# A decoder layer on one core: the first batches and the ternary weights get a list of steps of their own on each engine

## The reference

```python
# 1: linear attention without a denominator, 16 heads of 32
q, k, v = x @ Wq.T + bq, x @ Wk.T + bk, x @ Wv.T + bv
phi_q, phi_k = elu(q) + 1.0, elu(k) + 1.0
context = phi_q * cumsum(phi_k * v, axis=1) * 32 ** -0.5
x = layernorm(x + context @ Wo.T + bo)
# 2: attention over ctx, 32 query heads on 8 key heads of 16; ctx is keys and values
x = layernorm(x + softmax(qh @ kh.T / 4) @ vh)
# 3: feed-forward, 512 -> 2048 -> 512, each of its three products being
def h_bitlinear(x, w):
    xq = act_quant(fwht(x))      # Walsh-Hadamard, then 8 bits per token
    wq = weight_quant(w)         # scale = mean(|w|); round(w / scale) in -1, 0, 1, times scale
    return xq @ wq.T
x = layernorm(x + h_bitlinear(silu(h_bitlinear(x, w_gate)) * h_bitlinear(x, w_up), w_down))
```

## Time and profile before

| what | value |
|---|---|
| median of the runs | 1795.86 us |
| lowest and highest of three runs | 1795.64 and 1796.21 us |
| the profiled execution, its own time | 1794.42 us |
| its span, first to last instruction | 1792.6 us |
| PE busy | 1629.8 us (91% of the span) |
| DVE, ACT, POOL busy | 1379.0, 833.8, 186.6 us |
| granted PE clock, mean | 0.961 of full speed |
| one round of the cyclic order, steady | 100.36 us |
| issue of w_gate's transfer | 6.75 us after the start |

### The profile page before, as it was taken

One profiled execution on the slowest core, in us unless ns is written; L12 is line 12 of the kernel. 1 busy time (PEld: TensorE's weight loads), 2 busy tenths in 40 slices (PEclk: granted clock), 3 DMA queues, 4 the chain that ended last, 5 costly groups with the idle time before them and its releaser, 6 DMA issues.

```text
span 1792.6 us, 25396 instructions
## 1 busy us (share of the span) xinstructions
PE 1629.8 (91%) x10470; PEld 1006.7 (56%) x10470; DVE 1379.0 (77%) x1759; ACT 833.8 (47%) x784; POOL 186.6 (10%) x154
## 2 busy tenths in 40 slices
PE   7776699999999999999999999999999999996855
PEld 5443465655656565655656565655656565653534
DVE  3776897878869697878869697878879697877746
ACT  1134336363554545463544546463645536453623
POOL 0402502001020202010010202010010202010000
PEclk9886699999999999999999999999999999997978
DMA  5432220404050311404040311304040401304000
GB/s 206 64 99 106 38 19 19 63 19 62 2 80 1 62 19 30 52 20 62 2 80 1 71 11 33 48 19 63 9 73 1 74 8 40 42 7 60 7 6 12
DMA packets 100122, 75.73 MB, mean 42 GB/s; under 512 B 6044, under 2 KB 85148, under 8 KB 99496
## 3 DMA queue, kind: packets, MB, share of 16 engines
q1 hardware_dynamic: 100008, 74.10, 22.4%
...
## 4 chain that ended last, share of the span: by engine, by line
PE 81%; DVE 9%; ACT 7%; issue 2%; DMA 1%; SPq 0%; POOL 0%; POOLq 0%; ACTq 0%; DVEq 0%
PE psum L658 11%; PE psum L508 11%; PE psum L685 7%; PE psum L702 6%; PE psum L532 6%; PE psum L554 6%; PE psum L609 6%; PE psum L596 5%; PE psum L575 5%; ACT ffn_mem L733 3%; PE psum L677 3%; PE psum L638 2%; PE psum L542 2%; ACT qdT L733 2%; PE psum L694 2%
## 5 line engine op out<-in xcount | busy, mean ns | idle before, releaser
L736 ACT ACTIVATE attn_mem<-psum 128x1024 f32<-128x1024 f32 x256 | 254.8, 1023 | 137.3 <-PE psum L609 135.3
L1013 DVE TENSOR_REDUCE mneg<-psum 128x4 f32<-128x1024 f32 x256 | 303.6, 1218 | 14.1 <-PE psum L575 13.7
L733 ACT ACTIVATE ffn_mem<-psum 128x1024 f32<-128x1024 f32 x160 | 160.4, 1023 | 245.6 <-PE psum L677 100.6
L1144 POOL TENSOR_TENSOR grstd<-gvare,neg_half 128x1 f32<-128x1 f32 x32 | 18.2, 568 | 1376.3 <-DVE gvare L912 1376.3
L575 PE MATMUL psum<-kst,attn_mem 96*128 96x256 bf16 x1024 | 152.2, 277 | 7.6 <-DMA attn_mem<-q_dram 3.0
L609 PE MATMUL psum<-attn_mem,kst 98*128 98x512 bf16 x512 | 150.2, 390 | 7.6 <-ACT ffn_mem L733 2.9
L824 ACT ACTIVATE ffn_mem<-psum,sc 128x1024 f32<-128x1024 f32 x64 | 71.4, 1115 | 183.3 <-PE psum L658 183.1
L1105 DVE TENSOR_TENSOR ffn_mem<-ffn_mem 128x1024 f32<-128x1024 f32 x128 | 150.4, 1215 | 0.6
L685 PE MATMUL psum<-had,ffn_mem 128*128 128x128 f32 x1024 | 129.2, 280 | 16.5 <-ACT ffn_mem L733 16.5
L596 PE MATMUL psum<-attn_mem,vpad 128*32 128x256 f32 x2048 | 141.1, 394 | 3.3 <-ACT attn_mem L736 3.3
L685 PEld LDWEIGHTS psum<-had,ffn_mem 128*128 128x128 f32 x1024 | 121.9, 194 | 30.0 <-issue 18.1
(11 more groups left out here) (152 smaller groups left out, 2501.7 us busy)
## 6 DMA issues: line engine op xcount, KB each, us to landing
attn_mem<-q_dram SPq DMA_DIRECT2D x192, 128.0 KB, 6.7
...
x_in<-in_x SPq DMA_DIRECT2D x16, 512.0 KB, 3.9
...
ffn_mem<-in_L_ffn_w_gate SPq DMA_DIRECT2D x1, 4096.0 KB, 21.6
ffn_mem<-in_L_ffn_w_up SPq DMA_DIRECT2D x1, 4096.0 KB, 13.9
ffn_mem<-in_L_ffn_w_down SPq DMA_DIRECT2D x1, 4096.0 KB, 13.9
c_in<-in_ctx SPq DMA_DIRECT2D x16, 128.0 KB, 2.2
```

The source lines that it names most:

```text
L733: return nc.scalar.activation(dst, src, ACT.Copy)
L736: return nc.scalar.activation(dst, src, ACT.Exp, **kw)
L1013: nc.vector.tensor_reduce(mneg[:, h, t, GQ * g:GQ * (g + 1)], region(f"max{u}").rearrange("p (h t) -> p h t", h=GQ), AX_X, ALU.max, negate ...
```

## The change

`orders` is unchanged. Two tables of lists are new, `first_orders` and `last_orders`, and `all_batches` runs the cyclic order only for i = 3 to 15 between them. In `first_orders` an entry names its batch directly (`x_k.1+1` is batch 1, no suffix is batch 0); in `last_orders` it is counted from the last batch. All steps run exactly as often as before. `last_orders` spells out what the cycle did in rounds 16 to 19, in the same sequence on every engine. `first_orders` is another sequence than that of the rounds up to 2.

```diff
-    LEAD = 4
+        first_orders = {
+            "sp": """x_fetch t_load.0 x_fetch+1 x_split x_stack.0 t_load.1 x_stack.1 s_mT.0 t_load.2 s_mT.1 x_fetch+2 x_split+1
+                x_stack.0+1 x_stack.1+1 s_mT.0+1 s_mT.1+1""",
...
+            "dve": """t_abs.0 x_k.1 x_v.1 x_q.3 x_ctx x_o.1 x_norm t_sum.0 x_split t_quarter.0.0 x_q2 t_lower.0.1 t_quarter.0.1
...
+            "pool": """x_prep s_copy x_o.1""",
+        }
+        last_orders = {
...
-            for i in range(-LEAD, B + LEAD):
+            for entry in first_orders[engine].split():
+                n, name, args = parsed(entry)
+                steps[name](n, *args)
+            for i in range(3, 16):
                 for off, name, args in steps_of[engine]:
                     n = i + off
                     if n == 0 or (0 < n < B and name[0] != "t"):
                         steps[name](n, *args)
+            for entry in last_orders[engine].split():
+                off, name, args = parsed(entry)
+                steps[name](B - 1 + off, *args)
```

More of the change, by code:

```diff
@@ L192, in decoder_layer @@
                 s_copy-2 c_dn.0-3 c_dn.1-3""",
+        }
+        first_orders = {
+            "sp": """x_fetch t_load.0 x_fetch+1 x_split x_stack.0 t_load.1 x_stack.1 s_mT.0 t_load.2 s_mT.1 x_fetch+2 x_split+1
+                x_stack.0+1 x_stack.1+1 s_mT.0+1 s_mT.1+1""",
+            "pe": """x_load x_k.0 x_v.0 x_q.0 x_k.1 x_q.1 x_v.1 x_q.2 x_q.3 x_c x_o.0 x_o.1 t_sum.0 x_split x_load+1 x_kst.0 x_k.0+1
+                x_k.1+1 x_v.0+1 t_quarter.0.0 x_v.1+1 x_kst.1 s_max.0 t_quarter.0.1 s_max.1 s_max.2 s_max.3 s_max.4 s_max.5
+                s_max.6 s_max.7 x_q.0+1 s_mT.0 x_q.1+1 s_max.8 x_q.2+1 s_max.9 s_max.10 s_scores.0 x_q.3+1 t_quarter.0.2 x_c+1
+                s_scores.1 t_quarter.0.3 s_scores.2 x_o.0+1 s_scores.3 x_o.1+1 s_max.11 s_max.12 t_sum.1 s_pv.0 s_max.13
+                s_max.14 s_max.15 s_scores.4 s_scores.5 s_scores.6 s_pv.1 s_scores.7 s_mT.1 t_quarter.1.0 s_pv.2 t_quarter.1.1
+                s_pv.3 s_scores.8 s_scores.9 s_scores.10 s_scores.11 s_pv.4 s_scores.12 t_quarter.1.2 s_scores.13 s_scores.14
+                s_out.0 s_pv.5 s_scores.15 s_pv.6""",
+            "act": """x_load x_k.1 x_q.3 x_split x_load+1 x_q1 x_k.1+1 t_quarter.0.0 x_kst.0 x_kst.1 t_quarter.0.1 s_mT.0 s_scores.0
+                x_q.3+1 t_quarter.0.2 s_scores.1 t_quarter.0.3 s_scores.2 s_scores.3 s_scores.4 s_scores.5 s_mT.1 s_scores.6
+                t_quarter.1.0 s_scores.7 t_quarter.1.1 s_scores.8 s_scores.9 s_scores.10 s_scores.11 s_scores.12 t_quarter.1.2
+                s_scores.13 s_scores.14 s_scores.15 x_load+2 t_quarter.1.3 t_quarter.2.0 x_split+1 t_quarter.2.1 t_quarter.2.2
+                t_quarter.2.3 x_q1+1 d_hT x_k.1+2 x_kst.0+1 d_hx d_round d_qx c_gate.0 c_gate.1 c_gate.2 s_mT.0+1 c_gate.3
+                x_kst.1+1 x_q.3+2 c_dT.0.0""",
+            "dve": """t_abs.0 x_k.1 x_v.1 x_q.3 x_ctx x_o.1 x_norm t_sum.0 x_split t_quarter.0.0 x_q2 t_lower.0.1 t_quarter.0.1
+                x_k.1+1 t_lower.0.3 t_quarter.0.2 x_v.1+1 s_max.0 t_quarter.0.3 s_max.1 s_max.2 s_max.3 s_max.4 s_max.5 s_max.6
+                s_max.7 s_mT.0 s_max.8 s_max.9 x_q.3+1 x_ctx+1 s_max.10 t_abs.1 x_o.1+1 t_sum.1 s_max.11 s_pv.0 s_max.12
+                s_max.13 s_max.14 s_max.15 t_quarter.1.0 s_pv.1 t_lower.1.1 s_mT.1 t_quarter.1.1 t_lower.1.3 t_quarter.1.2
+                t_quarter.1.3 s_pv.2 s_pv.3 s_pv.4 s_out.0 s_pv.5""",
+            "pool": """x_prep s_copy x_o.1""",
+        }
@@ new lines, in decoder_layer @@
+        last_orders = {
+            "sp": """c_store.0-2 x_split x_stack.0 c_store.1-2 x_stack.1 s_mT.0 s_mT.1 c_store.0-1 c_store.1-1 c_store.0 c_store.1""",
+            "pe": """s_pv.7-2 x_load s_out.1-2 x_split-1 x_k.0 x_k.1 x_kst.0-1 d_hT-2 d_hx-2 x_v.0 x_v.1 d_qx-2 s_max.0-1 s_max.1-1
+                s_max.2-1 c_gate.0-2 s_max.3-1 c_up.0-2 s_max.4-1 c_gate.1-2 s_max.5-1 s_max.6-1 c_up.1-2 s_max.7-1 x_q.0
+                c_gate.2-2 c_up.2-2 x_q.1 s_mT.0-1 c_gate.3-2 x_kst.1-1 x_q.2 x_q.3 s_max.8-1 c_up.3-2 c_dT.0.0-2 s_scores.0-1
+                x_c s_scores.1-1 c_H.0.0-2 c_dT.0.1-2 s_max.9-1 c_H.0.1-2 s_max.10-1 s_scores.2-1 x_o.0 s_scores.3-1 x_o.1
+                s_max.11-1 c_dT.1.0-2 c_dT.1.1-2 s_max.12-1 s_pv.0-1 c_H.1.0-2 s_max.13-1 c_H.1.1-2 s_scores.4-1 s_max.14-1
+                s_scores.5-1 s_max.15-1 c_q.0-2 s_scores.6-1 s_mT.1-1 s_pv.1-1 c_dn.0-2 s_scores.7-1 s_pv.2-1 c_q.1-2 s_pv.3-1
+                s_scores.8-1 s_scores.9-1 s_scores.10-1 c_dn.1-2 s_scores.11-1 s_pv.4-1 s_scores.12-1 s_scores.13-1 s_pv.5-1
+                s_scores.14-1 s_out.0-1 s_scores.15-1 s_pv.6-1 s_pv.7-1 s_out.1-1 x_split x_kst.0 d_hT-1 d_hx-1 d_qx-1 s_max.0
+                s_max.1 s_max.2 c_gate.0-1 s_max.3 c_up.0-1 s_max.4 c_gate.1-1 s_max.5 s_max.6 c_up.1-1 s_max.7 c_gate.2-1
+                c_up.2-1 s_mT.0 c_gate.3-1 x_kst.1 s_max.8 c_up.3-1 c_dT.0.0-1 s_scores.0 s_scores.1 c_H.0.0-1 c_dT.0.1-1
+                s_max.9 c_H.0.1-1 s_max.10 s_scores.2 s_scores.3 s_max.11 c_dT.1.0-1 c_dT.1.1-1 s_max.12 s_pv.0 c_H.1.0-1
+                s_max.13 c_H.1.1-1 s_scores.4 s_max.14 s_scores.5 s_max.15 c_q.0-1 s_scores.6 s_mT.1 s_pv.1 c_dn.0-1 s_scores.7
+                s_pv.2 c_q.1-1 s_pv.3 s_scores.8 s_scores.9 s_scores.10 c_dn.1-1 s_scores.11 s_pv.4 s_scores.12 s_scores.13
+                s_pv.5 s_scores.14 s_out.0 s_scores.15 s_pv.6 s_pv.7 s_out.1 d_hT d_hx d_qx c_gate.0 c_up.0 c_gate.1 c_up.1
+                c_gate.2 c_up.2 c_gate.3 c_up.3 c_dT.0.0 c_H.0.0 c_dT.0.1 c_H.0.1 c_dT.1.0 c_dT.1.1 c_H.1.0 c_H.1.1 c_q.0 c_dn.0
+                c_q.1 c_dn.1""",
+            "act": """s_scores.0-1 s_scores.1-1 c_dT.0.1-2 c_H.0.0-2 c_H.0.1-2 s_scores.2-1 s_scores.3-1 c_dT.1.0-2 c_dT.1.1-2
+                c_round.0-2 c_H.1.0-2 c_H.1.1-2 s_scores.4-1 s_scores.5-1 c_q.0-2 s_mT.1-1 s_scores.6-1 c_round.1-2 s_scores.7-1
+                c_q.1-2 s_scores.8-1 s_scores.9-1 s_scores.10-1 s_scores.11-1 s_scores.12-1 s_scores.13-1 s_scores.14-1
+                s_scores.15-1 x_split x_q1 d_hT-1 x_kst.0 d_hx-1 d_round-1 d_qx-1 c_gate.0-1 c_gate.1-1 c_gate.2-1 c_gate.3-1
+                s_mT.0 x_kst.1 c_dT.0.0-1 s_scores.0 s_scores.1 c_dT.0.1-1 c_H.0.0-1 c_H.0.1-1 s_scores.2 s_scores.3 c_dT.1.0-1
+                c_dT.1.1-1 c_round.0-1 c_H.1.0-1 c_H.1.1-1 s_scores.4 s_scores.5 c_q.0-1 s_mT.1 s_scores.6 c_round.1-1
+                s_scores.7 c_q.1-1 s_scores.8 s_scores.9 s_scores.10 s_scores.11 s_scores.12 s_scores.13 s_scores.14 s_scores.15
+                d_hT d_hx d_round d_qx c_gate.0 c_gate.1 c_gate.2 c_gate.3 c_dT.0.0 c_dT.0.1 c_H.0.0 c_H.0.1 c_dT.1.0 c_dT.1.1
+                c_round.0 c_H.1.0 c_H.1.1 c_q.0 c_round.1 c_q.1""",
+            "dve": """s_pv.6-2 s_pv.7-2 x_norm-1 s_out.1-2 d_ln-2 x_split-1 d_norm-2 d_had-2 x_q2-1 d_hx-2 d_qx-2 x_k.1 x_v.1
+                s_max.0-1 s_max.1-1 s_max.2-1 s_max.3-1 c_up.0-2 s_max.4-1 s_max.5-1 s_max.6-1 c_up.1-2 c_fly.0.0-2 s_max.7-1
+                c_fly.0.1-2 c_up.2-2 c_fly.0.2-2 s_mT.0-1 c_fly.0.3-2 s_max.8-1 c_up.3-2 x_q.3 c_fly.1.0-2 x_ctx c_fly.1.1-2
+                s_max.9-1 c_fly.1.2-2 s_max.10-1 c_fly.1.3-2 c_H.0.1-2 x_o.1 s_pv.0-1 s_max.11-1 c_qd.0-2 s_max.12-1 s_max.13-1
+                s_max.14-1 s_max.15-1 c_H.1.1-2 s_mT.1-1 s_pv.1-1 c_qd.1-2 c_dn.0-2 s_pv.2-1 s_pv.3-1 c_norm.0-2 c_dn.1-2
+                s_pv.4-1 s_pv.5-1 s_out.0-1 c_norm.1-2 s_pv.6-1 s_pv.7-1 x_norm s_out.1-1 d_ln-1 x_split d_norm-1 d_had-1 x_q2
+                d_hx-1 d_qx-1 s_max.0 s_max.1 s_max.2 s_max.3 c_up.0-1 s_max.4 s_max.5 s_max.6 c_up.1-1 c_fly.0.0-1 s_max.7
+                c_fly.0.1-1 c_up.2-1 c_fly.0.2-1 s_mT.0 c_fly.0.3-1 s_max.8 c_up.3-1 c_fly.1.0-1 c_fly.1.1-1 s_max.9 c_fly.1.2-1
+                s_max.10 c_fly.1.3-1 c_H.0.1-1 s_pv.0 s_max.11 c_qd.0-1 s_max.12 s_max.13 s_max.14 s_max.15 c_H.1.1-1 s_mT.1
+                s_pv.1 c_qd.1-1 c_dn.0-1 s_pv.2 s_pv.3 c_norm.0-1 c_dn.1-1 s_pv.4 s_pv.5 s_out.0 c_norm.1-1 s_pv.6 s_pv.7
+                s_out.1 d_ln d_norm d_had d_hx d_qx c_up.0 c_up.1 c_fly.0.0 c_fly.0.1 c_up.2 c_fly.0.2 c_fly.0.3 c_up.3
+                c_fly.1.0 c_fly.1.1 c_fly.1.2 c_fly.1.3 c_H.0.1 c_qd.0 c_H.1.1 c_qd.1 c_dn.0 c_norm.0 c_dn.1 c_norm.1""",
+            "pool": """x_o.1-1 x_prep-1 d_ln-2 s_copy-1 c_dn.0-2 c_dn.1-2 x_o.1 x_prep d_ln-1 s_copy c_dn.0-1 c_dn.1-1 d_ln c_dn.0
+                c_dn.1""",
```

## The result

| what | before | after |
|---|---|---|
| median of three runs | 1795.86 us | 1817.41 us |
| lowest and highest | 1795.64 and 1796.21 us | 1816.64 and 1822.96 us |
| the profiled execution, its span | 1792.6 us | 1815.6 us |
| granted PE clock, mean | 0.961 | 0.955 |

The kernel after takes 1.0126 of the time before (95% interval 1.0112 to 1.0141): 21.6 us slower. The prediction was 1816 us, in a range of 1801 to 1824.

The account below looks back on a forecast made before the run. Head bound by PE waiting for ternary weights and at half clock, until sequences meet at batch 2's keys (210.22 us). `t_abs.2` 20.5 us later takes profiled 1794.4 to 1814.9; the median, 1.4 higher, gives 1816; range 1801 to 1824.

Parts of the forecast that it names:

- `t_abs.0` hidden: First absolute sum, moved ahead of batch 0's keys, runs under PE's projections at no cost; its 8.7 us afterwards go away.
- POOL takes DVE's turn: At POOL's next compare, released at 69.0, POOL goes before DVE's compare: POOL to 75.4, DVE's `t_lower.0.1` to 76.5.
- the other bound: DVE keeps its turn against POOL's compare, and what follows there comes 5.3 us earlier.
- `t_load.1` at 91.6: `t_quarter.0.3` ends at 91.6, so w_up's load is released then and not at 102.47, 11 us earlier.
- The queue behind w_up: Six q transfers issued behind w_up land after it, at 113; `s_max.8` starts then instead of 102.43, costing 10.6 us.
- From there to the third weight: From `s_max.8`: `x_o.1` ends at 136.5, `t_abs.1` hidden, POOL's second compare from 140.0, w_down issued at 163.
- The queue behind w_down: Rows of `s_mT.1` wait on SP and land behind w_down's 4 MB; `s_scores.8` starts at 178 instead of 153.78.
- The last stretch: From `s_scores.8` to `t_abs.2`: 14.5 us, putting `t_abs.2` at 192.5, 20.5 later than 171.98.
- Sum: Gain of 11 us at `t_load.1`, then queue costs, partly taken back by hiding `t_abs.1`: 20.5 us later in all, 1816 us.
- The first rival: On SP, transfers don't hold each other up, only late issue stays: 4 to 5 us gained, 1791 us; chance 0.12.
- The second: Rival: large transfers queue but 8 KB rows slip through, landing at 165: 7.5 us lost, 1803 us; chance 0.12.

Follow-up runs that it names:

- e1: The changed kernel with one step moved on SP, `s_mT.1` ahead of `t_load.2` again: 1802.21 us, ratio 1.0037.
- e9: e3 with `s_scores.8` ahead of `t_quarter.1.1` (PE, ACT), `s_scores.9` ahead of `s_pv.3` (PE), `s_pv.2` ahead of `t_quarter.1.3` (DVE): 1791.48 us, ratio 0.9983.
- e2: The changed kernel with one step moved on SP, `x_stack.1` ahead of `t_load.1` again: 1804.72 us, ratio 1.0054.
- e7b: The changed kernel with the six q transfers of `x_stack.1` issued from ACT's queue, released together with w_up: 1817.04 us, ratio 1.0116.
- e3: The changed kernel with two moves on SP, `x_stack.1` ahead of `t_load.1` and `s_mT.1` ahead of `t_load.2`: 1791.32 us, ratio 0.9978.
- e6: The changed kernel with w_down's transfer bringing one slice of 128 KB instead of 4 MB, same sequence: 1806.66 us, ratio 1.0058.

## Why the prediction held

- **`t_abs.0` hidden: right.** Sum at 28.54, POOL's first compare at 60.67 (predicted 60.7), `t_quarter.0.0` from 66.16 to 68.5 (predicted 66.4 to 68.8).
- **POOL takes DVE's turn: right in the profile of after, but not a property of the kernel.** DVE's compare took 6.46 us, to 76.0 (predicted 76.5). The timeline of DVE in after, and then in e1, whose DVE and POOL lists are the same:

```profile
69.56 6.46 DVE L788 TENSOR_SCALAR act_f<-ffn_mem,wnthr 128x2048 bf16<-128x2048 f32 x1
76.06 2.35 DVE L1030 SCALAR_TENSOR_TENSOR qdT<-ffn_mem,wthr,act_f 128x2048 bf16<-128x2048 f32 x1
```

```profile
69.43 1.28 DVE L788 TENSOR_SCALAR act_f<-ffn_mem,wnthr 128x2048 bf16<-128x2048 f32 x1
70.75 5.60 DVE L1030 SCALAR_TENSOR_TENSOR qdT<-ffn_mem,wthr,act_f 128x2048 bf16<-128x2048 f32 x1
```

  In e1 the compare was done at once and the difference behind it was held. That is worth 2.1 us (w_up at 87.13 against 89.19), not the 5.3 that I gave as the other bound.
- **`t_load.1` at 91.6: 2.4 us too late.** It left at 89.19, mainly since the second V half of batch 1 ran at full clock (80.72, 3.60 us) and not at half (5.2). In e9, where DVE's compare also took 6.47, this half took 5.13, V came 1.7 us later and w_up left at 90.89.
- **The queue behind w_up: right, with two sizes off that cancel.** w_up took 15.6 us and not 13.9, the q transfers another 5.5 and not 7.5; `s_max.8` came 21.1 us after the issue (predicted 21.4), at 110.31.
- **From there to the third weight: right, again with an error that cancels.** `x_o.1` ended 23.2 us later (predicted 23.5), `t_abs.1` was hidden, POOL's second compare started at 137.45 (140.0), w_down left at 162.45 (163). From that compare to w_down 25.0 us passed and not the predicted 23.0. Before it took 24.5, and the 1.5 us of waiting that the prediction took off were not saved.
- **The queue behind w_down: right.** `s_scores.8` 13.3 us after the issue, predicted 15.
- **The last stretch was mis-sized: 19.55 us against 14.5.** This is the largest error of the sum. The prediction took 14.5, between ACT's 10 and the 18.2 of before, and gave no sum for PE. It also misread before: the 18.2 us from 153.78 hold seven score groups (9 to 15) and two ternary copies, not eight. The windows of after show the clock (us; busy us of PE, PEld, DVE, ACT, POOL; PE clock; DMA; GB/s):

```profile
160.00:170.00 10.00, 1.93 (x16) 0.59 (x16) 3.11 (x3) 1.87 (x1) 0.00 (x0) 0.50 0.65 246
170.00:180.00 10.00, 2.92 (x7) 0.86 (x8) 0.00 (x0) 2.85 (x3) 0.00 (x0) 0.50 0.58 228
180.00:190.00 10.00, 8.42 (x55) 3.90 (x57) 0.58 (x2) 4.84 (x4) 0.00 (x0) 0.60 0.01 2
```

  PE came out of a pause of 11.9 us at clock 0.50, the lower of its two levels (1.2 GHz). PE's timeline has a group of 16 products of P·V on both sides of the rise:

```profile
180.78 1.94 PE L667 MATMUL psum<-attn_mem,vpad 128*32 128x256 f32 x16
...
189.74 1.07 PE L667 MATMUL psum<-attn_mem,vpad 128*32 128x256 f32 x16
```

  Six traces have the same steps in this stretch, `s_scores.8` to `t_abs.2`, with ACT busy for 9.74 us in each. It is longer the lower the clock was:

  | run | us | mean granted clock in it |
  |---|---|---|
  | e1 | 18.28 | 0.81 |
  | e2 | 18.71 | 0.79 |
  | after | 19.55 | 0.69 |
  | e7b | 20.42 | 0.63 |
  | e3 | 20.57 | 0.59 |
  | e6 | 22.33 | 0.51 |

  So PE's clock is worth about 4 us here, and PE's time comes in part on top of ACT's. That PE and ACT wait for each other by turns is how I explain it; no run could set the clock. Even the shortest of the six lies 3.8 us above 14.5. The 18.2 us of before, though of other steps, would have been the closer term: with it and the predicted start, `t_abs.2` would have been put at 196.2 and the time at 1820.
- **Sum.** The earlier parts came 2.2 us ahead of the forecast (175.78 for 178), the last stretch 5.05 behind: 195.33 against 192.5. The mechanism held, place by place; that the number is only 1.4 us off (1817.4 against 1816) is partly luck, since these two errors have opposite signs. By the traces' spans the change cost 23.0 us where the sum had 20.5, by the medians 21.6. From `t_abs.2` on nothing new happened: the matmuls of the second half of batch 2's keys came 23.3 us later (233.99 against 210.65).

The first rival (transfers don't hold each other up, 1791) fell with the two waits on PE. Its time is that of e3, where the transfers stand in no one's way (1791.32), but its places are not: it had w_down released at 152, in e3 it left at 148.14. The second (8 KB slip through) fell with 12.3 against 2.0 in e6.
